# A recurrence whose first two batches go in joint steps, and whose expert ranks, placements and scatters are moved within the steps

## What is computed

```python
x = x + attention(layernorm(x), ...)
x = x + ffn(layernorm(x), ...)            # first mixture of experts
x = x + recurrence(layernorm(x), ...)     # this stage
x = x + ffn(layernorm(x), ...)            # second mixture, whose routing is made in this stage

def recurrence(x, Wz, bz, Wh, bh, gamma, beta):
    k = x @ Wz + bz                       # z = sigmoid(k), keep = sigmoid(-k)
    g = x @ Wh + bh                       # g >= 0: g + 0.5, else sigmoid(g)
    # h[t] = keep[t] * h[t-1] + z[t] * value(g[t]), along the rows of one batch
    return layernorm(h) * gamma + beta + x

def ffn(x, router_w, ...):                # top 2 of 8 experts for every row
    topv, topi = top_k(softmax(x @ router_w.T), 2)
    ...
```

## Time and profile before

| | |
|---|---|
| three runs | 1420.23, 1422.24, 1410.85 us, median 1420.23 |
| the profiled execution | 1426.52 us |
| its span | 1424.8 us |
| busy, share of the span | PE 82%, DVE 81%, ACT 69%, POOL 69% |

### The profile page before, as it was taken

How to read it: one execution, slowest core, us unless ns; L and a number is a source line. 1 busy time by engine, 2 the same in 40 slices (tenths; PEclk the granted TensorE clock), 3 DMA queues, 4 the chain that set the end, 5 groups by cost and what they waited for, 6 DMA issues and landing times. The chain is left out here.

```text
span 1424.8 us, 38072 instructions
## 1 busy us (share of the span) xinstructions
PE 1164.5 (82%) x11689; PEld 984.9 (69%) x11689; DVE 1148.5 (81%) x3808; ACT 979.3 (69%) x2078; POOL 989.8 (69%) x1131
## 2 busy tenths in 40 slices
PE   5789999999999999999649999767666727999950
PEld 3657777777777777776549999746554527999950
DVE  5489999999999999997468888678888855888848
ACT  3588888888888888886136666567777735666620
POOL 5246688888888888876747777626888874777730
PEclk9699999999999999998669999978999967999965
DMA  7311111111111111110423333212232122333338
GB/s 204 101 49 46 41 59 54 62 63 64 53 59 54 62 64 63 57 47 17 138 75 107 106 104 105 79 52 68 78 84 79 56 63 78 106 107 105 98 105 280
DMA packets 99443, 117.19 MB, mean 82 GB/s; under 512 B 17784, under 2 KB 79792, under 8 KB 99248
## 3 DMA queue, kind: packets, MB, share of 16 engines
q1 hardware_dynamic: 70560, 73.57, 17.6%
q0 software_dynamic: 16896, 35.16, 7.2%
q10 hardware_dynamic: 11792, 6.05, 1.5%
HBM read 47.56 MB, written 41.51 MB: 63 GB/s over the span
## 5 line engine op out<-in xcount | busy, mean ns | idle before, releaser
L1151 DVE TENSOR_TENSOR ebuf<-score_banks,region 128x768 f32<-128x768 f32 x256 | 243.5, 951 | 19.1 <-PE score_banks L860 14.1
L1400 ACT ACTIVATE region<-ebuf 128x768 f32<-128x768 f32 x256 | 215.9, 860 | 24.2 <-DVE ebuf L1151 24.1
L1378 ACT CAST copied<-max_banks 128x768 bf16<-128x768 f32 x251 | 201.9, 804 | 14.3 <-PE max_banks L848 12.0
L1840 POOL DMA_INDIRECT choice_rows<-second_yo,second_xg x136 | 130.7, 961 | 68.1 <-PE second_by L1878 41.1
L1840 POOL DMA_INDIRECT choice_rows<-first_yo,first_xg x136 | 131.1, 964 | 62.1 <-PE first_by L1878 32.8
L1692 POOL DMA_INDIRECT expert_rows<-d_rows,a_d_index x112 | 128.4, 1147 | 28.7 <-issue 17.2
L903 PE MATMUL bankO<-region,vaug 128*32 128x256 f32 (+1 forms) x2048 | 111.9, 336 | 1.4 <-ACT region L1400 1.4
L851 PE MATMUL max_banks<-region_r 32*128 32x256 f32 x502 | 98.1, 387 | 12.0 <-DVE ebuf L1151 7.5
L1916 ACT ACTIVATE second_silu<-second_bgu,second_biases 128x256 f32<-128x256 f32 (+1 forms) x144 | 66.5, 462 | 59.3 <-issue 29.3
L824 PE MATMUL max_banks<-identb,region 128*128 128x128 bf16 x502 | 100.2, 225 | 4.9 <-ACT copied L1378 4.8
L1916 ACT ACTIVATE first_silu<-first_bgu,first_biases 128x256 f32<-128x256 f32 (+1 forms) x144 | 66.5, 462 | 54.9 <-issue 26.8
(11 more groups left out here) (368 smaller groups left out, 4436.6 us busy)
## 6 DMA issues: line engine op xcount, KB each, us to landing
region_r<-region_r SPq DMA_DIRECT2D x192, 128.0 KB
first_xg<-expert_rows SPq DMA_DIRECT2D x64, 132.0 KB
second_xg<-expert_rows SPq DMA_DIRECT2D x64, 132.0 KB
z_rows<-choice_rows SPq DMA_DIRECT2D x32, 256.0 KB, 2.9
c_rows<-choice_rows SPq DMA_DIRECT2D x16, 512.0 KB, 5.2
out<-xres ACTq DMA_DIRECT2D x16, 256.0 KB, 5.6
choice_rows<-first_yo,first_xg POOLq DMA_INDIRECT x136
choice_rows<-second_yo,second_xg POOLq DMA_INDIRECT x136
```

Of the source, the lines that this page charges most:

```text
L1151: nc.vector.tensor_tensor(ebuf[:, half_of_ebuf(c, j), :, :], score_banks[:, :, 0:BK], bias32[:, plain(j), :], ALU.add).then_inc(scores_fre ...
L1378: nc.scalar.copy(copied[:, 2 * j:2 * j + 2, :], banks_of_max(c, j)[:, :, 0:BK]).then_inc(maxed_free, 1)
L1400: nc.scalar.activation(p32[:, j % 4, :, :], ebuf[:, half_of_ebuf(c, j), :, :], ACT.Exp).then_inc(exped, 1)
L1840: pool.indirect_dma_start(choice_dram, bass.IndirectOffsetOnAxis(ap=xg[:, i % G, t, E:E + 1].bitcast(I32), axis=0), yo[:, i % 4, t, :], No ...
```

## The change

All of it is in `recurrence`. Batches 0 and 1 now go through the five stages in joint steps 0 to 4, so batch b from 2 on enters in step b-1, and there are 37 steps instead of 39. The norm tables grow from six to eight columns, and every reader takes its column by a function. The prologue of TensorE and the fifth step of ScalarE are written out by hand. TensorE's `back` is split into `residual`, `back` and `centre_of`.

For the routing of group m: the choice is in step 2m+5, in the same place of the step as before. TensorE ranks in that step too, behind `back` and `centre_of`. VectorE places at the head of step 2m+6, ahead of the statistics. POOL scatters the first choice ahead of the root of step 2m+6 and the second choice ahead of the root of step 2m+7; the late groups scatter their second choice behind the root. `scan` waits for the centring of the batch two before.

```diff
-        LAST = B + 7
...
+        LAST = B + 5
+        ENTER, GATE, SCAN, END, SEND = range(5)
+
+        def held(i, stage):
+
+            n = i - stage
+            return [0, 1] if n == 0 else [n + 1] if 1 <= n <= B - 2 else []
...
         def chosen_in(i):
+            return (i - 5) // 2 if i % 2 == 1 and 5 <= i <= B + 3 else None
+
+        def placed_in(i):
             return (i - 6) // 2 if i % 2 == 0 and 6 <= i <= B + 4 else None
-
-        def placed_in(i):
-            return (i - 7) // 2 if i % 2 == 1 and 7 <= i <= B + 5 else None
...
                 def scan(b, q, valued):
                     ch.wait(valued)
+                    if b >= 2:
+                        dve.wait_ge(c_full, b - 1)
...
                 for i in range(LAST):
                     q = i % 2
+                    if placed_in(i) is not None:
+                        place(placed_in(i))
                     if norms(i):
                         statistics(i, q)
                     if chosen_in(i) is not None:
                         dve.wait_ge(d_logits_taken, 2 * chosen_in(i) + 2)
                         d.sort(ch, chosen_in(i))
                         d.number(ch, chosen_in(i)).then_inc(d_compared, 1)
-                    if placed_in(i) is not None:
-                        place(placed_in(i))
...
                     if norms(i):
                         shifts(i, q)
-                    if scans(i):
-                        scan(i - 2, q, valued)
+                    if scanning:
+                        scan(scanning[0], scanning[0] % 2, valued)
+                    for b in scanning[1:]:
+                        valued = values(b, b % 2)
+                        scan(b, b % 2, valued)
                     if chosen_in(i) is not None:
                         choose(chosen_in(i))
-                    if ends(i):
-                        finish(i - 3, 1 - q)
+                    for b in held(i, END):
+                        finish(b, b % 2)
...
                 for i in range(LAST):
                     q = i % 2
+                    if placed_in(i) is not None:
+                        scatter(placed_in(i), 0)
+                    if i >= 7 and q == 1 and not d.late((i - 7) // 2):
+                        scatter((i - 7) // 2, 1)
                     if norms(i):
                         pool.wait_ge(ready, i + 1)
                         means_free(pool, i)
-                        lo, hi = held(i)
+                        lo, hi = columns(i)
                         nc.gpsimd.tensor_tensor(rs[:, q, lo:hi], arg[:, q, lo:hi], half[:, lo:hi], ALU.pow).then_inc(rooted, 1)
-                    if i >= 8 and q == 0 and not d.late((i - 8) // 2):
-                        scatter((i - 8) // 2, 1)
-                    if placed_in(i) is not None:
-                        scatter(placed_in(i), 0)
-                        if d.late(placed_in(i)):
-                            scatter(placed_in(i), 1)
+                    if placed_in(i) and d.late(placed_in(i)):
+                        scatter(placed_in(i), 1)
...
+                def rank(m):
+                    pe.wait_ge(d_chosen, m + 1)
+                    pe.wait_ge(d_logits_taken, 2 * m + 2)
+                    d.rank(ranks).then_inc(d_ranked, 1)
+
+                pe.wait_ge(added, 4)
+                for b in range(2):
+                    residual(b, b, tiles(b), True, False)
+                    residual(b, b, flat(beta[:]), False, False)
+                for b in range(2):
+                    turn_input(b, b)
+                for b in range(2):
+                    gates_of(b, b)
...
                 ranked = 0
...
+                for i in range(END, LAST):
+                    for b in held(i, SCAN):
+                        back(b, b % 2)
+                        centre_of(b, b % 2)
+                    if chosen_in(i) is not None:
+                        rank(chosen_in(i))
                         ranked += 1
...
+                    for b in held(i, ENTER):
+                        turn_input(b, b % 2)
+                    if i > SEND:
+                        for b in held(i, SEND):
+                            turn(b)
+                    for b in held(i, ENTER):
+                        gates_of(b, b % 2)
+                    if i > SEND:
+                        for b in held(i, SEND):
+                            router(b, ranked)
...
+                    early = i in (GATE, SCAN)
+                    if early:
+                        normalise(i + 1, i)
+                    for b in held(i, GATE):
+                        make_gates(b, b % 2)
+                    if i == SEND:
+                        for b in range(2):
+                            apply(b, i)
+                        norm_outputs(2, 0, i)
+                        for b in range(2):
+                            take(b)
+                        take_logits(0)
+                        normalise(5, i)
+                        take_logits(1)
+                        take_x(5, 1)
+                        for b in range(2):
+                            copy(b, i)
+                        continue
```

More of the change, by code:

```diff
@@ L2054, in recurrence @@
         wz, wh, cols, gamma, beta = (consts[n] for n in ("wz", "wh", "z_cols", "gamma", "beta"))
[L2055 to L2059, removed]
+        half = sb("z_half", [P, 8])
+        stats, mv = sb("z_stats", [P, 2, 8, 6]), sb("z_mv", [P, 2, 8, 2])
+        arg, rs = sb("z_arg", [P, 2, 8]), sb("z_rs", [P, 2, 8])
+        shift, dT = sb("z_shift", [P, 2, 8]), sb("z_dT", [P, 2 * P])
         d = Dispatch(nc, ctx, s, "z_", w, shares[1])
@@ L2298, in gates_of, with residual @@
                     nc.tensor.matmul(bk[q][:, S:2 * S], wh[:], xT[:, q, :], start=True, stop=True).then_inc(k_full, 1)
+                def residual(b, q, x, first, last):
+                    nc.tensor.matmul(bh[q][:, 2 * P:4 * P], ident[:], x, start=first, stop=last)
                 def back(b, q):
@@ L2335, in router @@
                     last.then_inc(d_logits_full, 1)
-                ranked = 0
-                for i in range(LAST):
-                    q = i % 2
-                    if placed_in(i) is not None:
-                        pe.wait_ge(d_chosen, ranked + 1)
-                        pe.wait_ge(d_logits_taken, min(2 * ranked + 3, B))
-                        d.rank(ranks).then_inc(d_ranked, 1)
-                        ranked += 1
-                    if scans(i):
-                        back(i - 2, q)
-                    if enters(i):
-                        turn_input(i, q)
-                    if sends(i):
-                        turn(i - 4)
-                    if enters(i):
-                        gates_of(i, q)
-                    if sends(i):
-                        router(i - 4, ranked)
+                def rank(m):
+                    pe.wait_ge(d_chosen, m + 1)
+                    pe.wait_ge(d_logits_taken, 2 * m + 2)
+                    d.rank(ranks).then_inc(d_ranked, 1)
@@ new lines, in _ @@
+                gates_of(2, 0)
+                back(1, 1)
+                for b in range(2):
+                    centre_of(b, b)
+                turn_input(3, 1)
+                gates_of(3, 1)
+                ranked = 0
+                for i in range(END, LAST):
[4 more added lines that the diff above has]
+                        rank(chosen_in(i))
+                        ranked += 1
+                    if i == SEND:
+                        for b in held(i, SEND):
+                            turn(b)
+                            router(b, ranked)
+                    for b in held(i, ENTER):
+                        turn_input(b, b % 2)
+                    if i > SEND:
+                        for b in held(i, SEND):
+                            turn(b)
+                    for b in held(i, ENTER):
+                        gates_of(b, b % 2)
+                    if i > SEND:
+                        for b in held(i, SEND):
+                            router(b, ranked)
@@ L2433, in _ @@
                 for i in range(LAST):
[L2434 to L2449 removed]
+                    if i > SEND + 1:
+                        for b in held(i - 1, SEND):
+                            take_logits(b)
+                    early = i in (GATE, SCAN)
[3 more added lines that the diff above has]
+                        make_gates(b, b % 2)
+                    if i == SEND:
+                        for b in range(2):
+                            apply(b, i)
+                        norm_outputs(2, 0, i)
+                        for b in range(2):
+                            take(b)
[3 more added lines that the diff above has]
+                        take_x(5, 1)
+                        for b in range(2):
+                            copy(b, i)
+                        continue
+                    for b in held(i, END):
+                        norm_outputs(b, b % 2, i)
+                    if not early:
+                        for b in held(i, ENTER):
```

(8 more changed lines are left out.)

99 lines of the change are left out of this document (42 added, 57 removed).

## The result

The changed kernel takes 1470.18 us (median of four runs, 1465.86 to 1473.95), the kernel before 1421.24. The ratio is 1.034, with a 95% interval of 1.030 to 1.038: 3.4% slower, where 2.5% was forecast (1456 us, whole range 1441 to 1472, the main case's own range 1450 to 1463). The profiled execution took 1465.86 us, with a span of 1464.1.

The account below looks back on a forecast made before the run. POOL's chain of 128 scatters and roots was taken as the bound: pairs, 13.74 + 2.97 - 0.41 = 16.3 us, and tail give +39.4, the start -3.5, net +35.9 us; median 1456, whole range 1441 to 1472.

Parts of the forecast that it names:

- main case: Whole kernel: POOL waits for the indices once a pair, median 1456 us, own range 1450 to 1463; chance 0.60.
- The loop: POOL, odd step's root to `scatter(m, 0)`: a wait of 3.17 us in place of 0.20, +2.97 us a pair.
- port rival: Moved scatter group on POOL: additions hold it up, so 0.41 us does not come back; +5.7 us, 1462; chance 0.14.
- clock rival: TensorE in the middle stretch: idles longer, gets 1.2 GHz; +0.6 us a pair, +8.5 us, 1465; chance 0.12.
- Steps 2 to 5 of the loop: Shift through TensorE's transposes and centring 1.55 us; rank to placement 0.31; placement to indices 1.00; indices to scatter 0.28.
- Step 1: From the end of POOL's odd-step root to the start of VectorE's shift: 0.03 us.
- VectorE stays covered by 0.8 us: Odd step: VectorE needs 6.0 us from its shift, POOL's four second-choice scatters and root take 6.85.
- The part that comes back: First-choice scatters on POOL no longer start beside a scan: 0.41 us a pair regained, pair 16.3 us.
- The tail: From `scatter(14, 0)` to the end of the last scatter on POOL: 22.3 us, where before it is 20.0.
- The start: Joint first steps: both scans 4.1 us early, then 25.2 us to the first scatter, at 965.5, 3.5 us early.
- a first scatter before 960 us: Sign of being wrong; the first scatter was expected to start between 963 and 969 us.
- Costed at nothing: Edits taken as off POOL's chain: `scan`'s wait for `c_full`, `router`'s wait for placement, rank's dropped wait for logits; no cost.

Follow-up runs that it names:

- e1_behind: Changed kernel with every POOL group of four scatters again behind the step's root, all else of the change kept: 1431.62 us, ratio 1.008.
- e4_place_late: Changed kernel with VectorE's placement behind the statistics again, scatters still ahead of the roots: 1502.95 us, ratio 1.058.
- e7_dose: Changed kernel with five useless statistics instructions (about 1.0 us) on VectorE between rank and placement: 1487.3 us, ratio 1.049.
- e8_dose_before: Kernel before the change with the same 1.0 us of useless VectorE work at the same place of its placement: 1419.6 us, ratio 1.001.
- e5_values_first: Changed kernel with VectorE's values ahead of sort and number in the odd step: 1467.28 us, ratio 1.035.
- e6_clock_held: Changed kernel with useless matmuls in `back` while TensorE waits for the scan, nine in even steps, two in odd: 1461.96 us, ratio 1.031.
- e2_joint_only: e1_behind with placement behind the statistics and rank at the head of the placing step, leaving the joint steps alone: 1418.47 us, ratio 0.999.
- e3_moves_only: Kernel before with placement at the step's head, rank behind `back`, scatters ahead of the roots, without joint steps: 1470.11 us, ratio 1.034.
- e9_rank_early: e1_behind with the placement alone back behind the statistics, the rank staying in the choice's step: 1422.45 us, ratio 1.001.
- e12_before_scan: Kernel before the change with VectorE's scan ahead of the shifts and nothing else: 1421.26 us, ratio 1.000.

## Why the prediction was right, and where its sum was short

**The loop is right, in place and sign.** The forecast was that `scatter(m, 0)` would wait for VectorE's indices directly behind the root of the odd step. The trace shows it in every pair, e1_behind removes it and 38.6 us with it, and a longer path inside it costs time in every turn (e4_place_late, e7_dose), where the same dose costs none without the loop (e8_dose_before). The time of 1470 us lies outside the main case's own range, 1450 to 1463, and inside the whole range only because that was drawn past the port and the clock rival; a part of each came true.

**Steps 2 to 5 of the loop** were 1.55, 0.31, 1.00 and 0.28 us; measured 1.58, 0.31, 0.99 and 0.30.

**Step 1, root end to shift, failed**: 0.03 us forecast, 0.51 measured in the pair shown, and 0.3 to 0.5 in most others (POOL's idle is 3.5 to 3.75 us, once 4.2). The idle of the fourteen pairs sums to 50.7 us for 44.4 forecast. Its base was the paragraph that VectorE stays covered by 0.8 us in the odd step. That counted VectorE's work (6.0 us) and left out the 1.4 us for which the sort waits for the logits. The cause is the one that the clock rival named, TensorE's lower level behind a longer idle time, in another place: I looked for it in the transposes and the centring of the loop, which come out at the full clock's 1.58 us, and priced it at 0.6 us a pair; it sits in the even step, in router and logits, and costs 0.5. e5_values_first and e6_clock_held both bring POOL's idle in most pairs to 3.17 us, the sum of the prediction's steps, the one by covering the wait and the other by removing it, though the time hardly follows. VectorE's idle ahead of `z_shift` shows the same: forecast at 2.6 us in the even steps and 0.8 in the odd ones, it is 3.05 in the even step of the pair shown and none in the odd one.

**The part that comes back was over-sized.** I took 0.41 us from the moved group. It now takes 1.14 + 0.96 + 1.13 + 0.96 us for 1.44 + 1.04 + 0.96 + 0.96 (by the earlier trace rows and the plain 0.96), 0.21 less; and the second-choice group gained a 1.05 in its second place. The additions cost the moved group 0.28 us, as e4_place_late shows by their absence. Thus the pair was forecast at 16.3 and measured at 16.9 to 17.2 us; the port rival's part of this is 0.2 to 0.3 us a pair. Over the 14 pairs, 1195.54 - 959.31 = 236.2 us for 226.2: these 10 us are what the sum lacked.

**The tail was right**: 22.3 us forecast, 1216.89 + 0.96 - 1195.54 = 22.3 measured.

**The start was right in size and wrong in cause.** The first scatter was forecast 3.5 us early and came 4.9 us early, reckoned from the first addition (38.6 for 43.5 us). I credited it to the joint steps. They bring 0.2 us (e2_joint_only), and the moves bring 4.3 us without them (e3_moves_only), mostly since the first placement no longer stands behind a step's statistics: from the last shift ahead of it to its start it is 1.9 us in e3_moves_only and 5.6 before. The joint steps do bring the second scan 5.5 us early (4.1 forecast), but with the routing in its old places the way from there to the first scatter takes 29.9 us (e2_joint_only), where the prediction put 25.2 and before it is 24.6. The changed kernel does take 25.2 us, with the help of the moves: the size was met by luck. The prediction also named a first scatter before 960 us as a sign of being wrong, and it starts at 959.31. That sign was set by the times of one profiled execution: the first addition comes 4.8 us sooner in the other, and reckoned from it the scatter is only 1.4 us ahead of the forecast (38.6 for 40.0).

**Costed at nothing**: the placement at the head of the step. Inside the loop it is in the sum. Once the loop is opened it costs 9 us of its own (e1_behind against e9_rank_early), which no part of the prediction names. It does not add to the result, as POOL's wait lies over it.

**Not settled**: the median went up by 48.9 us and the stage by 44.5 in the profiled executions (from the first addition to the last scatter: 297.2 for 252.6). The execution profiled before stood 5 us above its median and the one after 4 us below, and what differs outside the recurrence lies ahead of it (the first addition at 925.51 and at 920.68); no run here was made on that.

## What to carry to other kernels

When work is moved ahead of something on an in-order engine, write down what the moved instruction waits for, and follow that back to see whether it comes from the very instruction now queued behind or just ahead of it on the same engine; if so, the move closes a loop, and the engine pays the loop's whole length once per turn, however early the work stands in the program. An engine that is busy 83% of a stage and hardly ever waits for another (the rest is issue time) is the bound, and its queue should hold only work whose inputs were made a turn earlier. And when a cover of less than 1 us carries a sum, count the waits of the covering engine as well as its work, at the clock that the new idle times will leave.

## What the runs showed of the hardware

A first scatter is lengthened by a scan that is already running, not by one that starts just behind it. Before, the scan starts at 1022.91 and the scatter at 1022.99, and the scatter takes 1.45 us. Over all fourteen traces 157 first scatters start 0.07 to 0.09 us behind a scan, and all of them take 1.44 to 1.46 us. In e8_dose_before it is the other way about:

```profile
1041.48 1.03 POOL L2269 DMA_INDIRECT expert_rows<-z_second_rows,z_d_index  x1 [0.20 <-issue]
1041.51 0.69 DVE L2200 TENSOR_TENSOR_SCAN z_h<-z_keep,z_val 128x256 f32<-128x256 f32 x1
```

Here the scatter came 0.03 us first and took its plain 1.03 us. The Trainium skill (SBUF — State Buffer, section Who interferes with whom) calls the pair of ports that VectorE and GpSimd share an exclusive lock, and says that issue order decides who blocks; the two rows agree with that order. Of its rule that the additions with two SBUF inputs do the same, the trace shows only a part: the moved group's first scatter starts among four additions and takes 1.14 us, 0.11 more than the plain one, where the scan costs 0.41.

The other engine can be the one that pays. In e12_before_scan the product of the values, with two inputs, starts 0.05 us ahead of a scatter in both of these places:

```profile
1047.13 0.50 DVE L2194 TENSOR_TENSOR z_val<-z_gate,z_relu 128x256 f32<-128x256 f32 x1
1047.18 1.03 POOL L2266 DMA_INDIRECT expert_rows<-d_rows,z_d_index  x1 [0.20 <-issue]
...
1053.54 0.43 DVE L2194 TENSOR_TENSOR z_val<-z_gate,z_relu 128x256 f32<-128x256 f32 x1
1053.59 1.28 POOL L2266 DMA_INDIRECT expert_rows<-z_second_rows,z_d_index  x1 [0.20 <-issue]
```

In the first the product takes 0.50 us and the scatter its plain 1.03; in the second the product its plain 0.43 and the scatter 1.28. Wherever in these traces the product starts 0.03 to 0.07 us ahead, one of the two is long, and never both.

Matmuls without a use, on an engine that is not the bound, can take a wait off another engine: in e6_clock_held they raise TensorE's granted clock from 0.85 to 0.94 in the stretch from 970 to 1130 us, and the pairs in which it holds are at most 16.6 us long instead of 17.1. In the four pairs with 0.53 to 0.55 they are in the way.
